# A graph transformer layer on one core: layer one's running sums stored by an indexed DMA of GpSimd instead of a plain one of SP

## The reference, cut to what matters

```python
feat = (x @ W).reshape(n_nodes, H, D)
e = leaky_relu(el[src] + er[dst], 0.2)
m = segment_max(e, dst)
ex = exp(e - m[dst])
alpha = ex / segment_sum(ex, dst)[dst]
out = segment_sum(alpha[:, :, None] * feat[src], dst)
```

## Time and profile before

| what | value |
|---|---|
| median of three runs | 3248.05 us (3245.86 to 3252.17) |
| span of the profiled execution, first to last instruction | 3526.7 us; the page has no other time for it |
| busy in the span | DVE 2302.8, PE 2158.3, POOL 2134.4, ACT 1906.1 us |
| moved | 783.82 MB; 404.26 MB read, 378.13 MB written |
| DMA queues, share of 16 engines | q0 (POOL's) 33.2%, q1 (SP's) 29.1%, q10 2.4% |
| ring stores of layer one | 104 of 2,112 KB, by SP |

### The profile page before, as it was taken

One profiled execution on the slowest core, in us unless ns is written; L12 is line 12 of the kernel. 1 busy time (PEld: TensorE's weight loads), 2 busy tenths in 40 slices (PEclk: granted clock), 3 DMA queues, 4 the chain that ended last, 5 costly groups with the idle time before them and its releaser, 6 DMA issues. The chain is left out here.

```text
span 3526.7 us, 33756 instructions
## 1 busy us (share of the span) xinstructions
PE 2158.3 (61%) x7294; PEld 1353.6 (38%) x7294; DVE 2302.8 (65%) x5558; ACT 1906.1 (54%) x6229; POOL 2134.4 (61%) x2028
## 2 busy tenths in 40 slices
PE   6700455555544454544581006888898888888999
PEld 5600333333333332333361003544454444554565
DVE  7882788888988888888563235655466554665631
ACT  3300778787867667766462224544455444554532
POOL 3337677777767777764475666666666666666200
PEclk9855566666755555555796557989898998989999
DMA  6413899999989999998544465555565555555310
GB/s 230 122 21 103 312 338 345 341 348 337 374 330 364 369 345 358 364 348 318 156 127 116 151 226 186 163 167 177 177 190 160 171 173 174 188 171 169 136 33 12
DMA packets 244661, 783.82 MB, mean 222 GB/s; under 512 B 70282, under 2 KB 118253, under 8 KB 217801
## 3 DMA queue, kind: packets, MB, share of 16 engines
q0 software_dynamic: 127664, 369.53, 33.2%
q1 hardware_dynamic: 86715, 391.15, 29.1%
q10 hardware_dynamic: 30078, 20.99, 2.4%
HBM read 404.26 MB, written 378.13 MB: 222 GB/s over the span
## 5 line engine op out<-in xcount | busy, mean ns | idle before, releaser
L1514 POOL DMA_INDIRECT e_rows<-scratch_table,k_src x1664 | 1742.9, 1047 | 816.0 <-issue 400.3
L1624 DVE SCALAR_TENSOR_TENSOR e_ring<-e_ring,k_same,e_rows 128x520 f32<-128x520 f32 (+1 forms) x1560 | 967.6, 620 | 505.0 <-ACT e_rows L1647 179.0
L1647 ACT ACTIVATE e_rows<-e_rows 128x64 f32<-128x64 f32 (+1 forms) x4160 | 1196.9, 371 | 36.4 <-issue 24.9
L2251 PE MATMUL e_p_y<-e_wfo,e_h 128*121 128x256 f32 x1664 | 418.3, 407 | 116.4 <-DVE e_y L2013 67.6
L2251 PEld LDWEIGHTS e_p_y<-e_wfo,e_h 128*121 128x121 f32 x1664 | 325.8, 198 | 224.9 <-issue 128.5
L2225 PE MATMUL e_p_a<-e_xt,e_wf 128*128 128x484 f32 x832 | 387.4, 611 | 10.2 <-ACT e_h L2160 6.5
L2160 ACT ACTIVATE e_h<-e_p_a,e_shift,e_scale 128x484 f32<-128x484 f32 x208 | 151.9, 749 | 435.0 <-remote 282.5
L2237 PE MATMUL e_p_b<-e_h,e_wf 128*128 128x484 f32 x832 | 362.6, 578 | 13.8 <-ACT e_h L2160 11.5
L2013 DVE SCALAR_TENSOR_TENSOR e_y<-e_p_y,e_w,e_y 121x256 f32<-121x256 f32 x416 | 181.0, 476 | 248.5 <-PE e_p_y L2251 101.1
L1017 PE MATMUL e_p_kv<-e_wkv,nd_feat 128*121 128x512 f32 x208 | 190.0, 1066 | 107.2 <-DVE nd_feat L922 73.5
L1593 DVE TENSOR_TENSOR e_rows<-e_rows,e_shared 128x4096 f32<-128x4096 f32 x52 | 229.7, 4416 | 22.5 <-issue 8.9
(11 more groups left out here) (438 smaller groups left out, 3569.4 us busy)
## 6 DMA issues: line engine op xcount, KB each, us to landing
scratch_rows_a<-e_ring SPq DMA_DIRECT2D x104, 2112.0 KB
scratch_sums<-e_ring SPq DMA_DIRECT2D x104, 1032.0 KB
e_rows<-scratch_table,k_src POOLq DMA_INDIRECT x1664
scratch_table<-na_frow ACTq DMA_DIRECT2D x52, 245.8 KB
scratch_table<-hi_frow ACTq DMA_DIRECT2D x52, 124.8 KB
na_x<-in_x SPq DMA_DIRECT2D x13, 484.0 KB
e_wkv<-in_x SPq DMA_DIRECT2D x52, 121.0 KB
scratch_res<-e_wkv SPq DMA_DIRECT2D x52, 121.0 KB
```

What stands on the lines that cost most here:

```text
L1514: nc.gpsimd.indirect_dma_start(out=rows[:, n % B, g, :], out_offset=None, in_=table, in_offset=bass.IndirectOffsetOnAxis(ap=k.src[:, n * G ...
L1624: nc.vector.scalar_tensor_tensor(ring[:, i, j - c0, 0:W + H], prev, k.same[:, n * G + j:n * G + j + 1], rows[:, rb, j, 0:W + H], ALU.mult, ...
L1647: last = nc.scalar.activation(rows[:, rb, j, at], rows[:, rb, j, at], ACT.Copy, scale=rows[:, rb, j, W + h:W + h + 1])
L2251: last = nc.tensor.matmul(self.p_y[bank][0:BK, i * D:(i + 1) * D], self.h2[:, e % 2, kt, v:v + BK], self.wfo[:, e, kt, :], start=kt == 0, ...
```

## The change

The store of layer one moves from SP to POOL, as an indexed DMA with one index per lane. A lane in whose eight steps no target's edges end gets an index beyond the bound, and such a lane isn't written. The index of every lane and eight steps (`k.half`, 128 x 104) is made in `index_pass`: the eight values of `other` are added, and where they make eight, 4,000,000 is added to the row's place. (Lane 0 of the first eight steps is always stored.) Layer two is stored as before.

On POOL, store u (steps 8u to 8u+7) stands right behind the gather of step 8u+32; the last four stand behind all gathers. It waits for the same two semaphores as SP did. The rest renames: `HALVES` becomes slots of `HB` = 8 steps with `L.slot(u)` and `L.turns(u)`, still two of them, and the scratch tensor's type becomes int32 with views of it cast where it is read or written.

```diff
+STORE_AT = 32
@@ index_pass
+            nc.gpsimd.iota(home_i[:, :], [[RP // HB, Q], [1, HQ]], base=0, channel_multiplier=HQ).then_inc(iota_made, 1)
...
+            c(V.tensor_copy(home[:, :], home_i[:, :]))
...
+            c(V.tensor_reduce(inner_steps[:, :], other[:, :, :].rearrange(line).rearrange("p (u s) -> p u s", s=HB),
+                              AX.X, ALU.add))
+            c.done()
+            c(V.memset(inner_steps[0:1, 0:1], 0.0))
+            c.done()
+            c(V.tensor_scalar(inner_steps[:, :], inner_steps[:, :], HB - 0.5, NONE, ALU.is_gt, ALU.mult))
+            c.done()
+            c(V.tensor_tensor(k.half[:, :], home[:, :], inner_steps[:, :], ALU.add))
@@ edge_pass, sync
-                    sp.wait_ge(summed, n * G + c1)
-                    sp.wait_ge(dm_ready[i], n + 1)
-                    sp.dma_start(out[n // PB][:, n % PB * G + c0:n % PB * G + c1, :], ring[:, i, 0:c1 - c0, :]).then_inc(stored[i], 16)
+                    if L is L2:
+                        u, at = 2 * n + i, n % PB * G + i * HB
+                        filled(sp, u)
+                        sp.dma_start(out[n // PB][:, at:at + HB, :], ring[:, L.slot(u), :, :]).then_inc(stored[L.slot(u)], 16)
@@ edge_pass, gpsimd
+            homes = sums.rearrange("(u s) r -> u (s r)", s=HB)
+
+            def store(u):
+                filled(pool, u)
+                nc.gpsimd.indirect_dma_start(
+                    out=homes, out_offset=bass.IndirectOffsetOnAxis(ap=k.half[:, u:u + 1], axis=0),
+                    in_=ring[:, L.slot(u), :, :].rearrange("p s r -> p (s r)").bitcast(I32), in_offset=None,
+                    bounds_check=Q * RP // HB - 1, oob_is_err=False).then_inc(stored[L.slot(u)], 16)
...
+                    at = n * G + g - STORE_AT
+                    if L is L1 and at >= 0 and at % HB == 0:
+                        store(at // HB)
                     tails.pool(pool, n, g)
                     work.pool(pool, n, g)
+            if L is L1:
+                for u in range((T - 1 - STORE_AT) // HB + 1, NH):
+                    store(u)
             work.pool_last(pool)
```

More of the change, by code:

```diff
@@ L37 @@
 CW = 2 * (P + 1)
-HALVES = [(0, 8), (8, 16)]
-LENGTH = [c1 - c0 for c0, c1 in HALVES]
+HB = 8
+NH = T // HB
+HQ = NH // Q
+STORE_AT = 32
 GB = 13
@@ L60, in __init__, with slot, turns, stores @@
         self.act_heads = act_heads
-L1 = Layer("l1", 8, 512, 4, 2, 12)
-L2 = Layer("l2", 1, 256, 1, 3, 14)
+    def slot(self, u):
+        return u % self.halves
+    def turns(self, u):
+        return u // self.halves
+    def stores(self, u, slot):
+        return (u - slot + self.halves - 1) // self.halves
+L1 = Layer("l1", 8, 512, 4, 2, 12, 2)
+L2 = Layer("l2", 1, 256, 1, 3, 14, 2)
 def wait(eng, sem, value):
@@ L1460, in edge_pass, with row, filled @@
         block = s.block()
-        final = ring[:, 1, LENGTH[1] - 1, :]
+        def row(t):
+            return ring[:, L.slot(t // HB), t % HB, :]
+        def filled(eng, u):
+            eng.wait_ge(summed, (u + 1) * HB)
+            eng.wait_ge(dm_ready[L.slot(u)], L.turns(u) + 1)
         @block.sync
@@ L1480, in _ @@
                     er_load(n // PB + 1)
-                for i, (c0, c1) in enumerate(HALVES):
+                for i in range(2):
                     if i == 1:
@@ L1576, in head @@
                 ch.done()
-                wait(dve, dm_ready[1], n - 1)
+                last = 2 * (n - 2) + 1
+                if last > 0:
+                    dve.wait_ge(dm_ready[L.slot(last)], L.turns(last) + 1)
                 ch(nc.vector.tensor_tensor_scan(mext[:, b, :, :].rearrange(flat)[:, ::-1], rflat[:, 1:H * G1 + 1][:, ::-1],
@@ L1593, in _ @@
                     c(nc.vector.tensor_tensor(v, v, broad(share(b)[:, AH:H, 1:G1].rearrange("p h j -> p j h"), dim), ALU.mult))
-                wait(dve, stored[0], n * 16)
+                wait(dve, stored[L.slot(2 * n)], 16 * L.turns(2 * n))
                 wait(dve, summed, n * G)
+                first, before = row(n * G), row(n * G - 1)
                 if AH < H:
-                    c(nc.vector.tensor_tensor(ring[:, 0, 0, 0:W].rearrange(by_head, h=H),
-                                              ring[:, 1, LENGTH[1] - 1, 0:W].rearrange(by_head, h=H),
+                    c(nc.vector.tensor_tensor(first[:, 0:W].rearrange(by_head, h=H), before[:, 0:W].rearrange(by_head, h=H),
@@ L1605, in _ @@
                 c.done()
                 dve.wait_ge(scaled, n * G + 1)
-                nc.vector.tensor_tensor(ring[:, 0, 0, 0:W + H], ring[:, 0, 0, 0:W + H], rows[:, rb, 0, 0:W + H], ALU.add
+                nc.vector.tensor_tensor(first[:, 0:W + H], first[:, 0:W + H], rows[:, rb, 0, 0:W + H], ALU.add
                                         ).then_inc(summed, 1)
[L1610 to L1625, removed]
@@ new lines, in _ @@
+                for j in range(1, G):
+                    if j == HB:
+                        wait(dve, stored[L.slot(2 * n + 1)], 16 * L.turns(2 * n + 1))
+                    if j == L.ahead and n < NB - 1:
+                        head(n + 1)
+                    er_along(n, j)
+                    tails.vector(dve, n, j)
+                    work.vector(dve, n, j)
+                    if j == G - 1 and n:
+                        wait(dve, tails.kept, n // PB)
+                    t = n * G + j
+                    dve.wait_ge(scaled, t + 1)
+                    dve.wait_ge(summed, t)
+                    nc.vector.scalar_tensor_tensor(row(t)[:, 0:W + H], row(t - 1)[:, 0:W + H], k.same[:, t:t + 1],
+                                                   rows[:, rb, j, 0:W + H], ALU.mult, ALU.add).then_inc(summed, 1)
@@ L1642, in _ @@
                 act.wait_ge(wr_ready, n + 1)
[L1643 removed]
+                for i in range(2):
+                    u, c0, c1 = 2 * n + i, i * HB, (i + 1) * HB
                     for j in range(c0, c1):
@@ L1673, in hidden_pass @@
         prod = s.sb("prod", [P, 4, D])
-        rows = s.sb("rows", [BK, HB, L.row])
+        rows = s.sb("rows", [BK, RB_, L.row])
         rec = s.sb("rec", [BK, 2, KB, 8])
```

64 lines of the change are left out of this document (33 added, 31 removed).

## The result

The kernel with the change takes 3316.65 us (median of four runs, 3312.23 to 3320.17), the kernel before on the same chip 3250.11: a ratio of 1.0205 [1.019, 1.0219], 66.5 us slower. The forecast was 3220 with a range from 3155 to 3325; the time lies in the range, near the rival "POOL at its price" (3330), on the other side of no change. The range holds it only because it was drawn up to that rival; the forecast itself went the wrong way.

A forecast was written before the change was run, and what follows sets the result against it. In layer one's edge stage, DVE's order set the profiled pace, but DMA was taken to hold it outside the profile at 1306 us; with POOL the bound afterwards, 1278, 28 us less: 3220 us, range 3155 to 3325.

The forecast's parts named there:

- POOL at its price: Rival: GpSimd instructions cost the same outside the profile, 82 us more, 3330; chance 0.37 with its mild and dearer-store forms.
- From there to the median: Conversion from profiled to timed: layer one's edge stage 1306 us before, 1278 after, 28 us less, giving 3220.
- a median that rises while the profiled span does not: Sign for the whole run: the ratio taken for POOL, 0.921, is the step that failed.
- DMA as the hold of the stage: Layer one's edge stage outside the profile: DMA holds it at an assumed share of 0.97, 1306 us.
- The first paragraph on the bound: Layer one's edge stage: DMA full at 0.92, but transfers cost DVE only 38 us of 1377; DVE's order sets the pace.
- POOL's spare, 124 us: Layer one's edge stage: POOL without waits needs 1207 us of 1331, so 124 us are spare.
- The price of the store: POOL's indexed store: 1.18 us plus 0.30 gap, 1.48 us, including 0.16 for DVE's port lock; range 1.33 to 2.0.
- The bytes: Layer one's stores: 119 of 224.9 MB go, DMA share falls from 0.92 to 0.70, freeing 38 us of store waits.
- a share that stays above 0.8: Sign of being wrong: DMA share of layer one's edge stage above 0.8 instead of near 0.70.
- The new wait, the slot and the index pass: POOL's wait for step 8u+8 hidden with 3.6 us left; slot reuse hidden; six index-pass operations, under 2.5 us, hidden.
- POOL becomes the bound: Layer one's edge stage: 148 us of stores exceed 124 spare; last gather ends at 1668, stage 11 us later in profile.
- POOL still waiting over 60 us for steps: Sign of being wrong in layer one's edge stage: then DVE is the bound.

The follow-up runs named there:

- the ordinary execution: Kernel before, no edit, profiled a second time: 3250.58 us, profiled span 3248.7 us.
- the long one: Kernel before, unchanged, the first profiled execution, from which the prediction was read: span 3526.7 us.
- The wait alone: Kernel before, with POOL waiting for the step and the maxima at the new stores' places, no instruction behind the wait: 3252.03 us, ratio 1.0017.
- after less 100 gathers: Changed kernel without the gathers of steps 7 and 15 in every block but the first two: 3252.01 us, ratio 1.0016 against the kernel before.
- the later store: Changed kernel with each store behind the gather of step 8u+40 instead of 8u+32: 3380.35 us, ratio 1.0406 against the kernel before.

## Why the prediction failed, step by step

- *The step that failed is "From there to the median"*: "The stage is POOL's: 1388 us in profile time by its own ratio, which nothing in the trace tells. I take the whole run's, 0.921: 1278." POOL's ratio is 1: a gather takes 1119 ns in the ordinary execution and 1110 in the long one. Measured, the stage of after lasts from 316.5 to 1694.3, 1378 us, against the 1388 worked out in profile time; that of before lasts 1308 (314.2 to 1622.5), against 1306. (The prediction's window ends 3 us behind the last step.) The difference of the prediction's own figures at ratio 1, 82 us, is what it gave to the rival, and 66.5 came. The text also said which signs would mean this step: a median that rises while the profiled span does not; the span of 3526.7 became 3318.3 and the median rose.
- *DMA as the hold of the stage*, in the same part, was wrong as well. That its length of 1306 us came out is luck: the share was 0.95, as near 0.97 as one could ask, and half of the stored bytes could go for nothing. The first paragraph on the bound had it right: a full DMA is a bound only where somebody waits for it. The 34 us of the earlier trace rows were waits of that longer execution; in the ordinary one there are none in layer one.
- *POOL's spare, 124 us*, was mis-sized: it was read from the longer execution, in which POOL stood idle more. In the ordinary one it is 52. With that the prediction's own sum gives 1214 + 148 = 1362 us of POOL work, 96 past the end at 1266, less the 12 by which the lead can shrink: 84. Measured for the last step: 71.8, 69.5 when the later start (2.3 us) is taken off. The last gather ended 16 us earlier than by that sum: the store's 1.48 us were 1.09 + 0.30 = 1.39, 9 us for 100, and the gathers took 1099 ns instead of 1119, 16 us for 832; the 7 us of idle time and 2 of the small gathers go the other way. Nor is the spare one sum for the whole stage: none of the 52 us lies in the first 28 blocks, where 52 stores at 1.39 make 72 us, and there most of the loss came. In the long execution some 65 of the 124 us lay there.
- *The price of the store*: of 977 ns at least, 1017 in the median, 1504 at most, in after:

```profile
L1540 POOL DMA_INDIRECT scratch_rows_a<-e_ring,k_half x104: 977/1017/1504, 362.4 to 1695.1; - x104
```

  The low end (1.02 us), taken because it was nearest, was right, and the upper one, a price for each 4 KB piece, was wrong. Of the 0.16 us added for DVE's two-operand additions 0.07 shows in the mean (1.087 less the median of 1.017). By the two timelines, the 26 stores that begin under the block's scaling take 1.017 us on average, the 17 that begin under a step 1.29. The Trainium skill, "SBUF — State Buffer", section "SBUF: two separate sides", has a GpSimd instruction that reads SBUF shut out while such an operation runs; the trace agrees (1.29 against 1.017 us, at most 1.504), as the earlier trace rows did for the gathers. At 104 stores this comes to 7 us, not 17, an estimate from these durations.
- *The bytes*: 104.9 MB instead of 119. The prediction counted windows of eight steps without an end of a target; but `same` is 0 at the first slot of each lane, so that `other` is 0 at each lane's last slot and the last of the eight windows of a lane is always stored. 7/8 of the windows at 0.469 and 1/8 at one make 0.535, 120.4 MB stored; q0 gained 120.0. The share fell to 0.81, not to 0.70, so that one sign of being wrong, "a share that stays above 0.8", came as well. Neither moved the time: half the stored bytes fewer gave nothing, and storing all lanes changed it by 6 us, within the two intervals.
- *The new wait, the slot and the index pass*: hidden in the main, as forecast. The wait alone costs 5.6 us, and DVE waits 2.1 us for stores in after. Layer one's stage starts 2.3 us later in after (first gather at 316.5 instead of 314.2), but not for the six operations: with the same index pass it starts at 314.1 in after less 100 gathers and at 313.5 with the later store, and DVE's wait at the end of that pass is shorter by what they take (50.4 us instead of 53.0).
- *POOL becomes the bound*: right, in the signs that were named for it: the scatter at 1.09 us (1.2 was named), the last gather ended at 1662.7 (1668), no wait of POOL for steps beyond its gap before the last stores, DVE at the heads for gathers. The sign "POOL still waiting over 60 us for steps" was badly put: the 78.9 us in that row are 259 gaps of 0.3.

## What to carry to other kernels

A DMA share of 0.95 said nothing here of what fewer bytes are worth; ask which engine waits for a transfer, and for how long, in an execution as long as the timed one. An operation moved to another queue is priced by its instruction on the engine that takes it, against that engine's idle time less its gaps, and part by part of the stage: here 100 instructions of 1.39 us on an engine with 52 us to spare, all of them in the second half. Where the profiled execution is longer than the timed ones, its waits may be others while its instructions are as long as ever, as here: no engine's work is to be scaled by the ratio without a row that shows it, and a second profile is worth more than any argument about it.

## What the runs showed of the hardware that was not expected

- An indexed scatter cost POOL about the same whatever it carried: 1087 ns on average for rows of 16,896 bytes with some 47% of the lanes left out, 1068 with every lane stored, 1122 with 512-byte rows and every lane left out.
- The DMA engines' busy share wasn't proportional to what they moved. At 356 GB/s it was 0.95, with half the stored bytes 0.90 at 270, and after the change 0.81 at 262: at nearly the same rate, two shares.
- The page's count of bytes written to memory takes lanes that a scatter leaves out for written: 378.13 MB in after, with 104.9 MB left out, and 378.13 with every lane stored. The queues' counts don't.
- With POOL the engine that is waited for, eight gathers' difference in where the store stands made 64 us.
